# A ramp read from PSUM instead of SBUF in the two softmax passes of a four-layer graph network

## The reference

```
# layer 0: three rounds of weighted sums, then one softmax over ALL edges
for W in (W1, W2, W3): h = tanh((segment_sum(rel_w[type] * h[dst], src) + h) @ W)
e = leaky_relu((xh @ u1)[src] + (xh @ u3)[dst] + const);  alpha = softmax(e)
out = segment_sum(alpha * h[dst], src)
# layer 1: attention with 8 heads, softmax within each node
h = (x @ W).reshape(n, 8, 16)
e = leaky_relu(a_src[src] + a_dst[dst], 0.2)          # with a loop on every node
alpha = exp(e - segment_max(e, dst)) / segment_sum(...)
out = segment_sum(h[src] * alpha, dst) + bias
# layers 2 and 3: plain segment sums of gathered rows
```

## Time and profile before

| | |
|---|---|
| median of 3 runs | 8414.17 us (8405.2 to 8419.44) |
| the profiled execution | 8404.53 us, its span 8402.8 us |
| pass 1, first to last gather issued | 3759.1 to 4900.1 us of the span |
| pass 2, first to last gather issued | 4985.6 to 6127.2 us of the span |
| VectorE, TensorE, GpSimd busy | 5524.2, 4863.3, 6133.9 us |

### The profile page before, as it was taken

One profiled execution on the slowest core, in us unless ns is written; L12 is line 12 of the kernel. 1 busy time (PEld: TensorE's weight loads), 2 busy tenths in 40 slices (PEclk: granted clock), 3 DMA queues, 4 the chain that ended last, 5 costly groups with the idle time before them and its releaser, 6 DMA issues.

```text
span 8402.8 us, 83291 instructions
## 1 busy us (share of the span) xinstructions
PE 4863.3 (58%) x18373; PEld 3672.0 (44%) x18373; DVE 5524.2 (66%) x18601; ACT 1307.1 (16%) x3858; POOL 6133.9 (73%) x6205
## 2 busy tenths in 40 slices
PE   1444449955556556565666657777756666644444
PEld 1333337734334344343333335555545555633333
DVE  7755548866665666658888877777775555644444
ACT  1222227700000000013333321111120000100000
POOL 3777779877776777767777747777747777477776
PEclk9666659977777777776766765555557777855555
DMA  4222225511112111121111122222223333322212
GB/s 107 83 77 77 79 70 144 134 53 53 53 53 61 53 53 53 53 61 48 49 48 48 48 59 77 77 74 76 74 70 106 106 106 106 94 53 53 53 53 63
DMA packets 497194, 599.44 MB, mean 71 GB/s; under 512 B 116565, under 2 KB 387717, under 8 KB 496680
## 3 DMA queue, kind: packets, MB, share of 16 engines
q0 software_dynamic: 184928, 385.91, 17.8%
q1 hardware_dynamic: 308748, 206.79, 8.8%
q10 hardware_dynamic: 3020, 1.36, 0.1%
HBM read 505.75 MB, written 94.66 MB: 71 GB/s over the span
## 4 chain that ended last, share of the span: by engine, by line
POOL 48%; issue 19%; PE 16%; DVE 10%; DMA 5%; ACT 1%; DVEq 1%; POOLq 0%; SPq 0%; ACTq 0%
POOL RING L2075 22%; PE PS L1535 10%; POOL RING L2088 9%; POOL ROWD L2058 8%; POOL RING L2097 5%; PE PS L1532 3%; DMA RING<-TAB,IDX 3%; POOL RC L2097 3%; DVE RB L884 1%; DVE HN L882 1%; DMA ROWD<-RB,IDX 1%; DVE RC L518 1%; PE PS L1606 0%; DVE OH L870 0%; PE PS L1557 0%
## 5 line engine op out<-in xcount | busy, mean ns | idle before, releaser
L1535 PE MATMUL PS<-RB,RING 128*128 128x256 f32 x4836 | 1535.5, 479 | 912.0 <-DMA RING<-TAB,IDX 831.1
L2075 POOL DMA_INDIRECT RING<-TAB,IDX x1612 | 1532.8, 951 | 549.7 <-issue 460.1
L1535 PEld LDWEIGHTS PS<-RB,RING 128*128 128x128 f32 x4836 | 1105.7, 239 | 1341.5 <-issue 703.3
L884 DVE TENSOR_TENSOR RA<-RA,PS 128x256 f32 x1612 | 665.0, 413 | 680.5 <-PE PS L1535 658.8
L2088 POOL DMA_INDIRECT RING<-TABQ,IDX x806 | 896.7, 1113 | 276.5 <-issue 242.5
L2075 POOL DMA_INDIRECT RING<-TABN,IDX x830 | 785.1, 946 | 350.6 <-issue 239.9
L2058 POOL DMA_INDIRECT ROWD<-RB,IDX x830 | 835.5, 1007 | 265.4 <-issue 243.1
L2075 POOL DMA_INDIRECT RING<-TABM,IDX x830 | 785.0, 946 | 332.1 <-issue 252.6
L884 DVE TENSOR_TENSOR RB<-RB,PS 128x128 f32 x1660 | 465.3, 280 | 552.7 <-PE PS L1535 549.4
L1535 PE MATMUL PS<-OH,RING 128*128 128x128 f32 x2216 | 563.3, 391 | 407.5 <-DMA RING<-TABM,IDX 405.7
L867 DVE TENSOR_SCALAR RB<-IOTA,KEY,WE 128x256 f32<-128x256 f32 x1612 | 729.3, 453 | 103.6 <-ACT RA L1859 45.6
(11 more groups left out here) (429 smaller groups left out, 9403.2 us busy)
## 6 DMA issues: line engine op xcount, KB each, us to landing
RC<-in_edge_attr_dram SPq DMA_DIRECT2D x830, 64.0 KB
RING<-ROWD SPq DMA_DIRECT2D x201, 264.0 KB, 2.9
RB<-KRD SPq DMA_DIRECT2D x52, 512.0 KB
RA<-KRD SPq DMA_DIRECT2D x52, 512.0 KB
RING<-TAB,IDX POOLq DMA_INDIRECT x1612
ROWD<-RB,IDX POOLq DMA_INDIRECT x830, 2.3
RING<-TABN,IDX POOLq DMA_INDIRECT x830
RING<-TABM,IDX POOLq DMA_INDIRECT x830
```

The source lines that it names most:

```text
L884: v.tensor_tensor(sl, sl, sums_of(k, weighted), ALU.add).then_inc(s_ad, 1)
L1535: m = t_.matmul(sums_of(t, wide), rows, ramp, start=True, stop=True)
L2075: p.indirect_dma_start(GD[:, t % SLOTS, :], None, table, bass.IndirectOffsetOnAxis(ap=idx[:, t:t + 1], axis=0)).then_inc(s_ring[t // 4 % 1 ...
```

## The change

Two ramps are copied once into PSUM in f32: `IOTAP` (256 wide, bank 7) ahead of pass 1, `IOTAG` (128 wide, bank 3) ahead of pass 2. The scores L958, the one-hots L1016 and the one-hots L1245 read these as their first input. Their second input (`PB`, `KEY0`, `KEY1`) stays in SBUF, and the outputs stay where and what they were. To leave bank 7 alone, the products of the running maximum move into bank 6, one place for each in place of two by turns, and the first of them waits for the group before (`s_gm3 >= g`) in place of the one before that. Each engine's instructions keep their order; two copies are added on VectorE.

```diff
+        IOTAP, IOTAG = PS[7][:, 0:WN], PS[3][:, 0:WD]
...
             v.memset(ZG, 0.0).then_inc(misc.sem, misc.one("zg"))
+            v.tensor_copy(IOTAP, IOTA[:, :]).then_inc(misc.sem, misc.one("iota"))
...
-                    v.tensor_copy(RHS1[:, 128:144], PS[7][:, 0:16]).then_inc(misc.sem, misc.one())
+                    v.tensor_copy(RHS1[:, 128:144], PS[6][:, 0:16]).then_inc(misc.sem, misc.one())
...
-                v.scalar_tensor_tensor(out=junk[:, t % 2, :], in0=IOTA[:, :], scalar=KEY0[:, t:t + 1],
+                v.scalar_tensor_tensor(out=junk[:, t % 2, :], in0=IOTAP, scalar=KEY0[:, t:t + 1],
                                        in1=PB[:, bass.ds(w * WN, WN)], op0=ALU.is_equal, op1=ALU.mult,
...
-                    v.tensor_reduce(MR[:, g % 4:g % 4 + 1], PS[6][0:1, g % 2 * 128:g % 2 * 128 + 128], AX_X,
+                    v.tensor_reduce(MR[:, g % 4:g % 4 + 1], PS[6][0:1, 0:128], AX_X,
...
-                        v.tensor_tensor(MG[:, g:g + 1], MG[:, g - 1:g], PS[7][:, g % 2:g % 2 + 1], ALU.max).then_inc(s_gm3, 1)
+                        v.tensor_tensor(MG[:, g:g + 1], MG[:, g - 1:g], PS[6][:, 256:257], ALU.max).then_inc(s_gm3, 1)
...
-                    v.tensor_tensor((OHB, OHT)[a // 4 % 2][:, 0:b - a, :], IOTAB[:, :].unsqueeze(1).to_broadcast([128, b - a, WN]),
+                    v.tensor_tensor((OHB, OHT)[a // 4 % 2][:, 0:b - a, :], IOTAP.unsqueeze(1).to_broadcast([128, b - a, WN]),
                                     KEY0[:, a:b].unsqueeze(2).to_broadcast([128, b - a, WN]), ALU.is_equal).then_inc(s_ohb, 1)
...
             v.tensor_copy(AR, HN[:, :, 136:144]).then_inc(pre1.sem, pre1.one())
+            v.tensor_copy(IOTAG, IOTA[:, 0:WD]).then_inc(pre1.sem, pre1.one())
...
-                    v.tensor_tensor(OBR[:, t % 52:t % 52 + 4, :], IOTAB[:, 0:WD].unsqueeze(1).to_broadcast([128, 4, WD]),
+                    v.tensor_tensor(OBR[:, t % 52:t % 52 + 4, :], IOTAG.unsqueeze(1).to_broadcast([128, 4, WD]),
                                     KEY1[:, t:t + 4].unsqueeze(2).to_broadcast([128, 4, WD]), ALU.is_equal).then_inc(s_ob, 1)
...
                         t_.wait_ge(s_gmax, g + 1)
-                        if g >= 2:
-                            t_.wait_ge(s_gm3, g - 1)
-                        t_.matmul(PS[6][0:1, g % 2 * 128:g % 2 * 128 + 128], GM[:, g:g + 1], IDENT[:, :], start=True,
+                        if g:
+                            t_.wait_ge(s_gm3, g)
+                        t_.matmul(PS[6][0:1, 0:128], GM[:, g:g + 1], IDENT[:, :], start=True,
...
-                        t_.matmul(PS[7][:, g % 2:g % 2 + 1], ONES[0:1, :], MR[:, g % 4:g % 4 + 1], start=True,
+                        t_.matmul(PS[6][:, 256:257], ONES[0:1, :], MR[:, g % 4:g % 4 + 1], start=True,
```

More of the change, by code:

```diff
@@ L994, in group_step @@
                         v.wait_ge(s_gm3, g)
-                        v.tensor_tensor(MG[:, g:g + 1], MG[:, g - 1:g], PS[7][:, g % 2:g % 2 + 1], ALU.max).then_inc(s_gm3, 1)
+                        v.tensor_tensor(MG[:, g:g + 1], MG[:, g - 1:g], PS[6][:, 256:257], ALU.max).then_inc(s_gm3, 1)
                     else:
-                        v.tensor_copy(MG[:, 0:1], PS[7][:, 0:1]).then_inc(s_gm3, 1)
+                        v.tensor_copy(MG[:, 0:1], PS[6][:, 256:257]).then_inc(s_gm3, 1)
                 else:
@@ L1583, in _ @@
             t_.wait_ge(misc.sem, misc.at["gret"])
-            t_.matmul(PS[7][:, 0:16], RET, ADC[:, :], start=True, stop=True).then_inc(s_misc_t, 1)
+            t_.matmul(PS[6][:, 0:16], RET, ADC[:, :], start=True, stop=True).then_inc(s_misc_t, 1)
             for t in range(NT0 + LAG0 + LATE0 + GS):
```

## The result

| | before | after |
|---|---|---|
| median, runs | 8411.74 us (8405.2 to 8419.44), 4 | 8214.81 us (8195.09 to 8223.31), 4 |
| ratio, 95% interval | 1 | 0.9762 [0.9743, 0.9782] |
| profiled execution, its span | 8404.53, 8402.8 us | 8195.09, 8193.3 us |

The changed kernel is 197 us faster by the medians; 159 were forecast.

What follows compares the result with a forecast made beforehand. GpSimd's gathers, some held by VectorE instructions with two SBUF inputs, were taken to pace both passes. 90 + 70 − 1 = 159 us off 8404.5 gave 8245.5, or 8255 us against the median of 8414.2; range 8200 to 8330.

Steps and rivals of the forecast that it cites:

- first rival: Both passes: VectorE's waits for TensorE shrink and gathers stay the pace; 210 us less, 8204 us; chance 0.07.
- The cause: Both passes: a VectorE instruction with two SBUF inputs holds a gather's start; without holds at most 236 us less.
- The rule for a row of instructions: Pass 2: a gather starting inside a scan, one-hot and L1251 behind it, waits until the row ends, 2.02 us.
- The price of a PSUM read: Scores and one-hots: reading the ramp from PSUM costs 0 for all three edits.
- rival of 64 ns a read: Scores and one-hots: each ramp read costs 64 ns more; only 83 us less, 8331 us; chance 0.06.
- the slower case: Both passes: repeated ramp reads from one PSUM bank stream at half rate; 138 us more, 8552 us; chance 0.05.
- The hold stays: Both passes: the hold hangs on the second input alone or something else; only copies are added, 8415 us; chance 0.10.
- Who paces next: Both passes: VectorE becomes the pace, 1.300 us a tile in pass 1 and 1.277 in pass 2.
- term "90": Pass 1: 94.1 us of VectorE's gather waits go, 4 us left for late gathers, which makes 90 us.
- my subtraction's 1.300: Pass 1 without VectorE's gather waits: (1141.0 − 94.1) / 805 = 1.300 us a tile.
- term "70": Pass 2: of VectorE's 80.7 us of gather waits, 0.2 us in each of 52 chunks stay: 70 us gained.
- Layers 2 and 3 and all before pass 1 stay: Outside both passes: layers 2 and 3 and everything before pass 1 keep their times.

Runs made afterwards that it cites:

- the swapped one: Changed kernel with the inputs of all one-hots exchanged, key in SBUF first, ramp in PSUM second: 9367.84 us, ratio 1.0026, in the stretched condition.
- the kernel with all three edits: Changed kernel, L1263's weights read from PSUM, two VectorE copies dropped, L978's constant added by ScalarE: 8187.08 us, 0.9733; in the stretched condition 9330.74 us, 0.9983.
- repeated kernel before: The kernel before the change, unaltered, measured once more: 8409.60 us, ratio 0.9998.
- the first four experiments: Changed kernel with PSUM ramps only for scores (0.9967), only pass 1 one-hots (0.9885), only pass 2 one-hots (0.9912), or f32 ramps in SBUF (1.0001).
- the stretched condition: Times when the kernel before took 9420 or 9350 us in place of 8400 to 8411; the changed kernel took 9429.33 us, 1.0012.

## Why the prediction was right, and where it was short

Forecast 8255 us, measured 8214.8, inside the range of 8200 to 8330; the gain was 197 us where the sum had 159. The measured time lies below the 8225 to 8290 that the prediction gave as the forecast's own range, in the strip that it had added for its first rival (8204). So the cause and the next pace came out as said, but the size landed inside the range partly by luck.

**The cause: right.** A gather is held by a VectorE instruction that reads two tensors in SBUF, and let go when one of them lies in PSUM. It was read from three rows of a timeline, and the whole trace of the kernel before bears them out. In pass 1, 168 gathers start with more than 0.2 us of a one-hot L1016 left and 180 with as much of a score L958 left; 99% and 84% of them take more than 0.05 us over the 0.945, and the median excess is what was left less 0.13 us, for both. Of 105 that start so in the add L1032 none does. Three kernels with one of the reads changed each moved only their own pass, and the one with the ramp back in SBUF moved nothing. By the sentence of the Trainium skill ("SBUF — State Buffer", "Who interferes with whom") that `tensor_tensor` was not seen to stall such DMAs the change would have gained nothing; the runs contradict it, at 97 us for 201 `tensor_tensor` and 74 us for 208. They agree with the other sentence that the prediction takes from there, that `tensor_tensor` with both inputs in SBUF contends with GpSimd's reads.

**The rule for a row of instructions: half right.** The prediction took from one row that a hold lasts until the row of such instructions ends. The trace before has 46 gathers of pass 2 like that one: they start in the scan L1194 and are let in only at the end of L1251, 1.07 us late each, together 49 of the some 103 us of excess of the pass. But 101 gathers start in L1245 with the same L1251 right behind, and all are let in 0.13 us ahead of the end of L1245. L1251 has one tensor as input, so the rule of two SBUF inputs does not cover what it does behind the scan. What tells the two cases apart stays open.

**The price of a PSUM read: right, 0.** 476, 1217 and 671 ns against 477, 1217 and 672 (means of L958, L1016 and L1245). The rival of 64 ns a read falls, and with it the slower case. L1058 and L1378 were the right neighbours, L1360 the wrong one. The 62 cycles between the 58 and the 120 of the Trainium skill ("VectorE: DVE Perf Modes", section on the TRN2 errata) show in none of the three forms. The prediction's 1.04 us per 1000 elements stands in no row; the two one-hots before differ by 545 ns for 512 elements, 1.06 us per 1000.

**The hold stays: falsified** by the changed kernel itself, and the order of the inputs by the swapped one.

**Who paces next: right.** VectorE has no gather wait left in pass 1 and 0.4 us in pass 2, and gathers wait now and then for slots in the ring. In pass 1 the kernel with all three edits bears it out: one step of 0.23 us a group less on VectorE brought 5 us, and the waits for gathers came back. The step of the prediction that was mis-sized is how far VectorE could go:

- *Pass 1, term "90": measured 121.* Two parts. I left 4 us of gather waits, and none stayed (94.1). And I wrote that the waits for the running maximum stay at 54; they fell to 12.9 + 17.3 = 30.2 us. 94.1 + 24.1 = 118 of the 121. The missing 24.1 us are the error that counts. Pass 1 ran at 1.260 us a tile, under the forecast 1.29 to 1.31. The stretch of the earlier trace rows without a gather wait, 1.27 us a tile, already lay closer to this than my subtraction's 1.300: I cited it as agreement, and should have asked why it was faster.
- *Pass 2, term "70": measured 78.* I left 10 us of gather waits, and 0.4 stayed. A chunk took 20.3 us, at VectorE's own 20.3; the 52 L1141 start from 4890.8 to 5926.0, one each 20.30 us. The mean of the gathers, 977 ns, is in the forecast 965 to 1000. The excess that is left comes to some 25 us, against the 0.5 us in each of 52 chunks, 26 us, of the prediction. Nearly all of it, 20.6 us, is of the 100 gathers that start in L1263; the scans, which the prediction named first, keep 1.4 us.
- *"Layers 2 and 3 and all before pass 1 stay": −6.4 and −4.2 us.* The repeated kernel before was 6.2 us longer ahead of pass 1 than the first one, and 2.7 us in layers 2 and 3, so this is about the size of the scatter between executions.

**The first rival, gathers stay the pace,** was half right about pass 1, and its 8204 us is nearer to the measured time than the forecast's 8255. It said that the running maximum's waits shrink as phases move, and they nearly halved; but the pace stayed above the 1.251 us of a free gather, at 1.260, with gathers waiting for VectorE and not the other way round.

**Why these waits shrank is open.** The shared bank is at most a small part: with it and the ramps in SBUF they are 14.3 + 34.0 us, against 54.3 and, in the repeated kernel before, 51.6. With the scores alone in PSUM they are 45.1, with the one-hots of pass 1 alone 38.3. TensorE's granted clock looked like a candidate. Two stretches of 50 us of the changed kernel (columns as above):

```profile
4150.00:4200.00 50.00, 31.64 (x97) 20.11 (x96) 46.94 (x162) 18.46 (x50) 37.81 (x41) 0.82 0.22 55
4350.00:4400.00 50.00, 34.48 (x91) 21.28 (x89) 45.84 (x159) 18.85 (x51) 36.93 (x40) 0.66 0.22 55
```

In the first, at 0.82, L997 never waits for TensorE; in the second, at 0.66, it waits once, for 1.3 us. Averaged over the pass the clock is 0.75 in the changed kernel and where only the one-hots of pass 1 read PSUM, and 0.70 to 0.72 in the kernel before and in the other three of the first four experiments. But the link does not hold up over more stretches. Over all 19 stretches of 50 us from 3800 to 4750 us the correlation of clock and waits is only −0.26, and in the repeated kernel before it is 0.13. And at the same clock, 0.73 to 0.77, a stretch of the kernel before has 2.1 us of these waits on average, one of the changed kernel 0.9. So the clock is not the main reason. More likely VectorE, no longer held up by gathers, comes to these steps at another time; no run here tests that.

## What to carry to other kernels

When an engine's instructions have a median at their undisturbed time and a mean well above it, look in the timeline at what runs on the neighbour while one of the long ones starts. If the excess follows that neighbour's instructions, it can perhaps be taken away there, here at no measurable cost, by moving one constant input of frequent VectorE instructions to PSUM. One long row is not a rule; go through all of them. Rank the candidates by how long each instruction holds, not by their number: 201 one-hots gave 93 us and 806 scores 32. And size the gain by the engine that comes next, in a stretch of the old trace in which it was not made to wait; a difference between that stretch and the average less its known waits is a term of its own.

## What the hardware showed beyond expectation

**The hold works the other way too.** VectorE's `tensor_scalar` L1254, SBUF to SBUF in bf16, got slower when the gathers of its pass were let go: before, the two groups of L1251 were

```profile
L1251 DVE TENSOR_SCALAR OHB<-RA,COLS 128x512 bf16<-128x512 bf16 x104 | 36.1, 347 | 0.0
L1251 DVE TENSOR_SCALAR OHT<-RA,COLS 128x512 bf16<-128x512 bf16 x104 | 35.6, 343 | 0.0
```

and after, with the instruction unchanged,

```profile
L1254 DVE TENSOR_SCALAR OHB<-RA,COLS 128x512 bf16<-128x512 bf16 x104 | 43.2, 416 | 0.0
L1254 DVE TENSOR_SCALAR OHT<-RA,COLS 128x512 bf16<-128x512 bf16 x104 | 39.3, 378 | 0.0
```

10.8 us of VectorE's time in all. The timeline of the changed kernel (start us, us, engine, line, operation) shows one:

```profile
5304.86 0.67 DVE L1248 TENSOR_TENSOR RA<-PS,KEY 128x512 bf16<-128x512 f32 x1
5304.90 0.94 POOL L2100 DMA_INDIRECT RING<-TABG,IDX  x1 [0.30 <-issue]
...
5305.44 0.51 DVE L1254 TENSOR_SCALAR OHB<-RA,COLS 128x512 bf16<-128x512 bf16 x1
5305.88 0.29 DVE L1279 TENSOR_TENSOR RB<-RB,PS 128x146 f32 x1
```

The gather starts 0.04 us into the one-hot and is not held, 0.94 us; before, a gather that started in this one-hot was held until the one-hot ended. L1254 takes 0.51 us here in place of 0.34. That it starts while a gather runs is not enough: 189 of 208 did so before, with a mean of 344 ns. It is when it starts. In the changed kernel 86 of 208 take more than 0.4 us, and all of them start 0.5 to 0.7 us into a gather and end about 0.11 us after that gather; the 56 that start in a gather's first 0.35 us take 0.33 to 0.35 us. Before, only 6 took more than 0.4 us, probably because a gather that was held until the one-hot ended was let in just as L1251 came. In pass 2 some of the conflict changed sides rather than went away. The two engines seem to share something that one of them holds at a time, while the other waits; a gather seems to need it in a later part of its course as well.

**Free gathers are worth nothing in the stretched condition.** There the changed kernel took 1.0012 [1.0003, 1.0021] of the time of the kernel before, with gathers of 944 and 966 ns. A saving of 2.4% that is steady at one time can be absent at another, for a cause that these profiles do not show.
